# A relational graph layer with a routed FFN: 23 of its 1614 gathered tiles brought row by row by SyncE, x and its table moved in longer runs, and the selection begun before the last FFN block

## The reference

```
hx   = einsum('ni,rio->rno', h, weight)
agg  = segment_sum(hx[edge_type, src], dst)
x    = x + agg * sqrt(0.5) + h_bias + (h @ loop_weight) * sqrt(0.5)
z    = layernorm(x);   w = z @ wr + br
sel  = the 3124 nodes of largest w
y    = gelu(z @ w1 + b1) @ w2 + b2
out  = x + z + (y * w at the nodes of sel, 0 elsewhere)
```

## Time and profile before

| | us |
|---|---|
| median of 3 runs (lowest, highest) | 2587.57 (2576.79, 2591.49) |
| the profiled execution | 2560.34 |
| its span, first to last instruction | 2558.7 |
| first gather of GpSimd starts | 69.90 |
| first sum of TensorE starts | 84.99 |
| DVE's first step of the selection | 2498.37 |
| TensorE, GpSimd, DVE, ACT busy over the span | 1869.3, 1548.9, 776.9, 697.8 |

### The profile page before, as it was taken

The page is one execution under the profiler, slowest core; times in us unless marked ns, Lnnn a source line. Parts: engine busy times, 40 slices in busy tenths (PEclk is TensorE's granted clock), DMA queues, the critical chain, the costliest instruction groups (busy, mean ns, idle before and its releaser), DMA issues.

```text
span 2558.7 us, 25060 instructions
## 1 busy us (share of the span) xinstructions
PE 1869.3 (73%) x8680; PEld 1529.2 (60%) x8680; DVE 776.9 (30%) x1714; ACT 697.8 (27%) x1341; POOL 1548.9 (61%) x1737
## 2 busy tenths in 40 slices
PE   1237878777877877887877877877877877877881
PEld 0126657666665665665666666756656665666671
DVE  6112322232232232232232232232232232222337
ACT  5102223223222222222322322223223223223240
POOL 2666666666666666666666666666666666666500
PEclk9568888887887898887988988888988887887895
DMA  7533333333333333333333333333333333333315
GB/s 254 158 88 98 98 99 95 93 103 97 97 103 95 97 101 97 96 100 97 99 103 97 97 105 97 98 102 99 97 103 98 98 103 97 95 101 96 85 33 179
DMA packets 126598, 265.50 MB, mean 104 GB/s; under 512 B 30091, under 2 KB 73003, under 8 KB 126473
## 3 DMA queue, kind: packets, MB, share of 16 engines
q0 software_dynamic: 79168, 218.05, 29.6%
q1 hardware_dynamic: 47304, 45.83, 5.7%
HBM read 244.52 MB, written 19.25 MB: 103 GB/s over the span
## 4 chain that ended last, share of the span: by engine, by line
PE 55%; another core or an unknown queue 21%; issue 10%; ACT 8%; DVE 3%; DMA 1%; SPq 1%; DVEq 0%; POOL 0%; ACTq 0%; POOLq 0%
PE bank L642 21%; PE bank L670 13%; PE bank L688 7%; PE bank L696 7%; PE bank L652 4%; ACT hidden L541 2%; ACT stage L506 2%; PE bank L672 2%; ACT L541 1%; DMA acc<-in_edge_type 1%; DVE acc L1060 1%; ACT L528 1%; DMA w_sb<-in_L_ffn_w 1%; ACT normed_t L533 1%
## 5 line engine op out<-in xcount | busy, mean ns | idle before, releaser
L404 POOL DMA_INDIRECT messages<-normed_table,gather_rows x1614 | 1531.0, 949 | 854.3 <-issue 433.3
L642 PE MATMUL bank<-messages,onehot 128*128 128x256 f32 x3228 | 929.3, 423 | 124.9 <-issue 100.6
L642 PEld LDWEIGHTS bank<-messages,onehot 128*128 128x128 f32 x3228 | 642.6, 213 | 248.9 <-issue 179.0
L919 DVE SCALAR_TENSOR_TENSOR sums<-bank,regular,sums 128x256 f32 x538 | 259.9, 483 | 1657.4 <-remote 850.8
L506 ACT ACTIVATE stage<-bank 128x256 f32<-128x256 f32 x538 | 207.3, 388 | 1737.4 <-remote 1013.9
L652 PE MATMUL bank<-ident,stage 128*128 128x128 f32 x1076 | 234.4, 297 | 254.8 <-issue 158.8
L670 PE MATMUL bank<-rel_sb,closed 128*128 128x256 f32 x1568 | 361.6, 384 | 8.7 <-ACT closed L512 8.7
L652 PEld LDWEIGHTS bank<-ident,stage 128*128 128x128 f32 x1076 | 151.5, 152 | 336.1 <-issue 283.1
L688 PE MATMUL bank<-normed_t,w_sb 128*128 128x128 f32 x1568 | 240.0, 316 | 131.2 <-ACT normed_t L533 72.2
L670 PEld LDWEIGHTS bank<-rel_sb,closed 128*128 128x128 f32 x1568 | 302.3, 193 | 53.3 <-ACT closed L512 10.8
L688 PEld LDWEIGHTS bank<-normed_t,w_sb 128*128 128x128 f32 x1568 | 225.4, 229 | 147.1 <-ACT normed_t L533 85.6
(11 more groups left out here) (136 smaller groups left out, 519.8 us busy)
## 6 DMA issues: line engine op xcount, KB each, us to landing
messages<-normed_table,gather_rows POOLq DMA_INDIRECT x1614
normed_x<-normed_table SPq DMA_DIRECT2D x49, 128.0 KB
residual<-resid SPq DMA_DIRECT2D x49, 128.0 KB
x_block<-in_x SPq DMA_DIRECT2D x48, 128.0 KB
node_out<-acc SPq DMA_DIRECT2D x12, 512.0 KB
messages<-in_x POOLq DMA_DIRECT2D x6, 896.0 KB, 14.9
normed_table<-messages SPq DMA_DIRECT2D x6, 896.0 KB, 8.0
messages<-residual SPq DMA_DIRECT2D x6, 896.0 KB, 10.1
```

Source lines behind the costliest of these rows:

```text
L404: pool.indirect_dma_start(messages[0:EP, g % RING, j * D:(j + 1) * D], None, table, bass.IndirectOffsetOnAxis(ap=gather_rows[0:EP, g, j:j ...
L642: last = nc.tensor.matmul(banks[g % STAGES][:, 0:D], onehot[0:EP, g % SLOTS, j, :], messages[0:EP, slot, j * D:(j + 1) * D], start=(j == 0 ...
L919: V.scalar_tensor_tensor(sums[:, :, to], banks[TURNS[g % 2]][:, 0:D].rearrange("p (n m) -> p n m", m=W), regular[:, 0:1], sums[:, :, to], ...
```

## The change

Four edits are made together.

1. In 23 groups (every second closing group, from `closes[3]` to `closes[47]`) GpSimd issues two gathers instead of three. The third tile is brought by SyncE into `row_messages` (two buffers): `bring_rows` loads the tile's 128 indices, reads eight at a time into registers, and issues one transfer of 1 KB for each row; 64 rows stand ahead of `normed_x` in each of two successive blocks. TensorE waits for 128 transfers before the third product.
2. x and the table are moved with partition-major chunks, 7 rows in a run (7 KB) instead of 1 (1 KB). The table's content is the same.
3. `src` alone is loaded by SyncE, at once; `dst` and `edge_type` are loaded by GpSimd behind x, ahead of its constants. `index_stage` stands behind all chunks.
4. The selection starts when the last `w_all` is there. TensorE's FFN of the last block stands in pieces between the rounds' count products, and `ffn_leave` of that block behind the eighth round.

```diff
@@ top of the program
+    row_tiles = [closes[2 * k + 3] for k in range((NB - 3) // 2)]
+    row_tile_of = {g: k for k, g in enumerate(row_tiles)}
...
-        table_chunks = table.rearrange("(c v p) d -> c p v d", p=P, v=CH)
+        table_chunks = table.rearrange("(c p v) d -> c p v d", p=P, v=CH)
...
+        row_list = sb("row_list", [1, P], I32)
+        row_messages = sb("row_messages", [P, 2, D])
@@ SyncE
-            sp.wait_ge(pads_set, 3)
-            for a, to in ((dst, dst_s), (src, src_s), (edge_type, type_s)):
...
+            sp.wait_ge(pads_set, 1)
+            sp.dma_start(src_s[:, 0:full_tiles, :], src[0:full_tiles * P * GE].rearrange("(t p e) -> p t e", p=P, e=GE)).then_inc(src_in, 16)
...
+            def bring_rows(k, half):
+
+                first = row_tiles[k] * GE + (J - 1) * EP
+                if half == 0:
+                    sp.dma_start(row_list[0:1, :], src[first:first + P].rearrange("(o p) -> o p", o=1)).then_inc(row_list_in, 16)
+                    sp.wait_ge(row_list_in, 16 * (k + 1))
+                    if k >= 2:
+                        sp.wait_ge(summed, row_tiles[k - 2] + 1)
+                for p in range(half * P // 2, (half + 1) * P // 2, LOAD):
+                    registers = [sp.alloc_register(f"row{k}_{p + n}") for n in range(LOAD)]
+                    sp.load(registers, row_list[0:1, p:p + LOAD])
+                    for n in range(LOAD):
+                        row = sp.snap(registers[n], donate=True, min_val=0, max_val=N - 1)
+                        sp.dma_start(row_messages[p + n:p + n + 1, k % 2, :], table[bass.ds(row, 1), :]).then_inc(rows_in[k % 2], 16)
...
             for b in range(1, NB):
+                if (b - 1) // 2 < len(row_tiles):
+                    bring_rows((b - 1) // 2, (b - 1) % 2)
                 sp.wait_ge(loop_turned, b)
@@ GpSimd
-            x_chunks = x[0:(NCH - 1) * CH * P, :].rearrange("(c v p) d -> c p v d", p=P, v=CH)
+            nc.gpsimd.memset(closed_rows[P - 32:P, 0:CH, :], 0.0).then_inc(node_pad_set, 1)
+            x_chunks = x[0:last_first * P, :].rearrange("(c p v) d -> c p v d", p=P, v=CH)
...
+            for a, to in ((dst, dst_s), (edge_type, type_s)):
+                pool.dma_start(to[:, 0:full_tiles, :], a[0:full_tiles * P * GE].rearrange("(t p e) -> p t e", p=P, e=GE)).then_inc(edges_in, 16)
...
-                for j in range(J):
+                for j in range(J - (g in row_tile_of)):
                     pool.indirect_dma_start(messages[0:EP, g % RING, j * D:(j + 1) * D], None, table,
@@ ACT
-                    act.wait_ge(edges_in, 16 * 9)
+                    act.wait_ge(src_in, 16 * 3)
@@ TensorE
-                pe.wait_ge(gathered[slot], 16 * J * (g // RING + 1))
+                brought = sum(1 for t in row_tiles if t <= g and t % RING == slot)
+                pe.wait_ge(gathered[slot], 16 * (J * (g // RING + 1) - brought))
                 for j in range(J):
+                    tile = messages[0:EP, slot, j * D:(j + 1) * D]
+                    if j == J - 1 and g in row_tile_of:
+                        k = row_tile_of[g]
+                        pe.wait_ge(rows_in[k % 2], 16 * P * (k // 2 + 1))
+                        tile = row_messages[0:EP, k % 2, :]
...
             for r in range(8):
+                if r < 2:
+                    ffn_first(NB - 1, r * HC // 2, (r + 1) * HC // 2)
+                elif r >= 4:
+                    ffn_second(NB - 1, (r - 4) * HC // 4, (r - 3) * HC // 4)
                 pe.wait_ge(counts_in, r + 1)
@@ VectorE
-                dve.wait_ge(edges_in, 16 * 9)
+                dve.wait_ge(edges_in, 16 * 6)
...
-                if c == 2:
-                    index_stage()
+            index_stage()
             window_stage()
...
-            dve.wait_ge(ffn_done, 2 * NB + 1)
+            dve.wait_ge(ffn_step, FFN_STEPS * NB)
...
                 radix_round(4 + r, key_lo[:, :], 12 - 4 * r)
+            ffn_leave(NB - 1)
...
+            dve.wait_ge(ffn_done, 2 * NB + 1)
             for b in range(NB):
```

More of the change, by code:

```diff
@@ L83, in gnn_ffn_program @@
     assert len(closing) == NB and NG % 2 == 0 and all(closes[b] + LEAVE < closes[b + 2] for b in range(NB - 2))
+    row_tiles = [closes[2 * k + 3] for k in range((NB - 3) // 2)]
+    row_tile_of = {g: k for k, g in enumerate(row_tiles)}
+    assert len(row_tile_of) == len(row_tiles)
     SELECTED = max(1, int(0.5 * N)) - 1
@@ L209, in gnn_ffn_program @@
         consts = sem("consts")
+        src_in = sem("src_in")
         edges_in = sem("edges_in")
@@ L243, in gnn_ffn_program @@
         gathered = [sem(f"gathered{i}") for i in range(RING)]
+        row_list_in = sem("row_list_in")
+        rows_in = [sem(f"rows_in{i}") for i in range(2)]
         onehot_ready = sem("onehot_ready")
@@ L281, in gnn_ffn_program @@
         written = sem("written")
+        full_tiles = NG_FULL // P
+        rest = NG_FULL - full_tiles * P
+        last_first = (NCH - 1) * CH
+        last_whole = (N - last_first * P) // CH
+        last_rest = N - last_first * P - last_whole * CH
         block = ctx.enter_context(nc.Block())
@@ L286, in _ @@
         def _(sp):
-            full_tiles = NG_FULL // P
-            rest = NG_FULL - full_tiles * P
-            sp.wait_ge(pads_set, 3)
-            for a, to in ((dst, dst_s), (src, src_s), (edge_type, type_s)):
[L292 to L295, removed]
+            sp.wait_ge(pads_set, 1)
+            sp.dma_start(src_s[:, 0:full_tiles, :], src[0:full_tiles * P * GE].rearrange("(t p e) -> p t e", p=P, e=GE)).then_inc(src_in, 16)
+            sp.dma_start(src_s[0:rest, full_tiles, :], src[full_tiles * P * GE:NG_FULL * GE].rearrange("(p e) -> p e", e=GE)).then_inc(src_in, 16)
+            sp.dma_start(src_s[rest:rest + 1, full_tiles, 0:E - NG_FULL * GE],
+                         src[NG_FULL * GE:E].rearrange("(p e) -> p e", p=1)).then_inc(src_in, 16)
             sp.dma_start(loop_sb[:, :, :], loop_w.rearrange("(k p) o -> p k o", p=P)).then_inc(loop_in, 16)
@@ L639, in sum_group @@
                     pe.wait_ge(onehot_ready, g // 2 + 1)
-                pe.wait_ge(gathered[slot], 16 * J * (g // RING + 1))
+                brought = sum(1 for t in row_tiles if t <= g and t % RING == slot)
+                pe.wait_ge(gathered[slot], 16 * (J * (g // RING + 1) - brought))
                 for j in range(J):
+                    tile = messages[0:EP, slot, j * D:(j + 1) * D]
[3 more added lines that the diff above has]
+                        tile = row_messages[0:EP, k % 2, :]
                     last = nc.tensor.matmul(banks[g % STAGES][:, 0:D], onehot[0:EP, g % SLOTS, j, :],
-                                            messages[0:EP, slot, j * D:(j + 1) * D], start=(j == 0), stop=(j == J - 1))
+                                            tile, start=(j == 0), stop=(j == J - 1))
                 last.then_inc(summed, 1)
@@ L681, in ffn_turn, with ffn_first @@
                 last.then_inc(ffn_turned, 1)
[L683 to L686, removed]
+            def ffn_first(b, first=0, past=HC):
+                if first == 0:
+                    pe.wait_ge(ffn_norm_t, b + 2)
+                    pe.wait_ge(ffn_done, 2 * b + 1)
+                for m in range(first, past):
                     for k in range(KC):
@@ L690, in ffn_first, with ffn_second @@
                                                 start=(k == 0), stop=(k == KC - 1))
[L691 to L695, removed]
+                if past == HC:
+                    last.then_inc(ffn_up, 1)
+            def ffn_second(b, first=0, past=HC):
+                if first == 0:
+                    pe.wait_ge(ffn_gelu, b + 2)
+                for m in range(first, past):
                     last = nc.tensor.matmul(banks[5][:, 0:D], hidden[:, m, :], w2_sb[:, m, :],
                                             start=(m == 0), stop=(m == HC - 1))
-                last.then_inc(ffn_down, 1)
+                if past == HC:
+                    last.then_inc(ffn_down, 1)
             pe.wait_ge(rel_in, 16 * KC)
@@ L714, in _ @@
                     loop_turn(closing[g - LOOP])
-                if g - UP in closing:
+                if closing.get(g - UP, NB - 1) < NB - 1:
                     ffn_first(closing[g - UP])
-                if g - DOWN in closing:
+                if closing.get(g - DOWN, NB - 1) < NB - 1:
                     ffn_second(closing[g - DOWN])
             for r in range(8):
+                if r < 2:
+                    ffn_first(NB - 1, r * HC // 2, (r + 1) * HC // 2)
+                elif r >= 4:
+                    ffn_second(NB - 1, (r - 4) * HC // 4, (r - 3) * HC // 4)
                 pe.wait_ge(counts_in, r + 1)
@@ L1002, in _ @@
                     ffn_normalize(closing[g - NORM])
-                if g - LEAVE in closing:
+                if closing.get(g - LEAVE, NB - 1) < NB - 1:
                     ffn_leave(closing[g - LEAVE])
-            dve.wait_ge(ffn_done, 2 * NB + 1)
+            dve.wait_ge(ffn_step, FFN_STEPS * NB)
```

18 lines of the change are left out of this document (11 added, 7 removed).

## The result

| | before | after |
|---|---|---|
| median, us (lowest, highest, runs) | 2586.26 (2576.79, 2591.49, 4) | 2848.07 (2843.07, 2859.53, 4) |
| the profiled execution, us | 2560.34 | 2848.06 |
| its span, us | 2558.7 | 2846.4 |
| TensorE's mean granted clock | 0.844 | 0.826 |

The account below looks back on a forecast made before the run. The prediction took GpSimd's gather issue plus a nearly fixed number of pauses, with TensorE held while gathers flow, as the bound. 28.9 + 7.5 + 9 = 45.4, scaled 45.9: 2587.6 - 45.9 = 2542 us, range 2525 to 2600.

Parts of the forecast that it names:

- The bound of before: Loop: TensorE held while gathers flow; GpSimd's issue, 1614 x 1.256 us, plus 197 pauses adding 324.5 us, together 2352 us.
- first rival: Loop: TensorE alone paces it, so fewer gathers free nothing; 2571 us, chance 0.25.
- 23 gathers, 28.9 us: Loop, GpSimd's side: 23 gathers fewer at 1.256 us each save 28.9 us, 0 if TensorE alone paces.
- SyncE hidden at 28.5 us a block: Loop, SyncE's side: 64 rows take 28.5 us of a 47.6 us block; normed_x comes 6.5 us late, hidden.
- my own bound: Loop, SyncE: the rows stay hidden as long as one costs less than 0.65 us all in.
- the backlog row: SyncE: a one-row transfer behind a backlog took 1.98 us, giving at most 127 us for a block's rows.
- Third rival: Loop: a row costs SyncE over 0.65 us; at 1 us, 69 us a block, 970 us more; chance 0.04.
- Second rival: Loop: rows in flight keep up the hold on TensorE, lengthening 118 pauses by 189 us; 2731 us, chance 0.18.
- Start, 7.5 us: Program start: shorter ACT waits bring the first gather and sum earlier; 7.5 us taken, bounds 0 and 11.
- both waits of 8.33 and 2.60: Start, ACT's path: 8.33 us waiting for DVE in the index stage, 2.60 us for the edge types, to go.
- End, 9: Tail: selection starts at the last w_all instead of 10.4 us later; 9 us gained, bounds 6 and 10.4.
- the sum of 45.4 us: Whole kernel: gain of 28.9 for gathers, 7.5 for the start and 9 for the tail, scaled to 45.9.

Follow-up runs that it names:

- rows_32_4: Changed kernel with 11 row tiles instead of 23, 32 rows a block: 2565.9 us, 0.992 at the slower level; 0.982 at the faster.
- dropped: Changed kernel with the 23 tiles brought by nobody, their third product taking the second tile's rows: 2142.3 to 2143.1 us, 0.976 at the faster level.
- no_rows_4: Changed kernel without its first edit, GpSimd making all 1614 gathers: 2564.0 us, 0.992 at the slower level; 0.988 to 0.989 at the faster.
- rows_only: Kernel before with the first edit alone, start and end as before: 2166.8 us, 0.987 at the faster level.
- after_3: Changed kernel, unaltered, run again beside the kernel before: 2142.0 us, 0.976 at the faster level.

## Why the prediction was wrong, by its steps

- **The bound of before.** Right that TensorE is held while gathers flow: without gathers its block falls from 48 to 34 us, and the clear condition shows a loop in which only GpSimd's 1.256 us a gather counts. The reading "GpSimd's issue time plus a nearly fixed number of pauses" wasn't shown for the held condition: 11 gathers fewer gave nothing (rows_32_4). That fits the first rival, TensorE with its holds as the pace, but 32 slow rows a block were in the same run, and the 23 gathers alone weren't measured held.
- **23 gathers, 28.9 us.** 26.4 to 28.2 clear (dropped). Held not seen.
- **SyncE hidden at 28.5 us a block.** This is the step that failed. The undisturbed cost was nearly right: 32.4 us for 64 rows (0.41 a row, 0.78 a load in place of the 0.596 of DVE's). Held, it is 51.9 us and 3.4 for the rest, over the block of 48.15, so that `normed_x` comes late and TensorE waits for it. By my own bound all of it stays hidden up to 0.65 us a row, with 4.8 us for the loads beside it; measured are 51.9/64 = 0.81 with the loads in it, and about 0.71 with 8 x 0.78 us for them taken out. The upper end was as real: 121.7 us for the first half tile, 127 by the backlog row.
- **Why it failed.** I had seen that TensorE's results are held for up to 15 us, and took the hold to be TensorE's own. It reaches a run of SyncE's instructions too: a register check of 37 ns takes up to 1.4 us. The rows that I priced by were single instructions: those of the program's start, where no gather runs, and the 0.32 us of the earlier trace rows. That second one does stand amid gathers, and so do 139 transfers of SyncE in the kernel before, from 186.8 us to the last gather, of which none took over 0.333 us. For `normed_x`:

```profile
L334 SPq DMA_DIRECT2D normed_x<-normed_table x48: 319/320/327, 186.8 to 2437.0; - x48
```

  So the trace on record had rows from within the stretch, and they spoke for my price. It held no close run of SyncE instructions there, and TensorE, with 8680 matmuls the engine with by far the most instructions, was the one held. One instruction's time didn't price 64 in a row, and the far bound deserved more than 0.04. That the closeness of the instructions makes the difference is read from these rows; no run tests it by itself.
- **Third rival** (a row over 0.65 us, chance 0.04): the mechanism that happened, at 0.71 and not 1 (0.81 with the loads). Its law overshoots little: 46 x (55.3 - 48.15) = 329 us, for 307.8 measured from the first to the last store. **Second rival** (2731, 0.18) had a time nearer to the result and, by rows_32_4, the wrong mechanism for nearly all of the loss. The range of the prediction reached neither.
- **Start, 7.5 us.** 13.8 earlier at the first gather, over my upper bound of 11. ACT is done with x 13.1 us earlier (its last `closed` starts at 42.87 in place of 55.96): both waits of 8.33 and 2.60 are gone whole, the first chunk of x is there 1.06 us sooner (DVE starts at 9.60 in place of 10.66), and ACT no longer waits for the constants, so the 2 us counted for them weren't lost (GpSimd's six issues of x took 3.40 us in place of 5.84). The DMA engines didn't set the rest. Whether all of it lasts when held isn't told: no_rows_4 gains 20.4 with 9.8 of the end in it, within 15 to 26 by its interval.
- **End, 9.** 9.8 us (9.6 by the stretch behind the last gather, 96.2 in rows_only and 86.6 in no_rows).
- **By condition.** Clear, the sum of 45.4 us was measured as 52.2: the gathers gave a little less than their term, start and end 23.8 to 25.7 in place of 16.5. On the condition of its own trace it was wrong by sign.

The Trainium skill's rule to coalesce small transfers ("DMA: Bandwidth & Descriptors", Rules for kernel authors), which I weighed and set aside, pointed the right way in the held condition; in the clear one 64 rows a block cost nothing. The 2.0 us of the page are a fit to transfers that GpSimd issues (Anatomy of one DMA); from row to row SyncE needed 0.41 us undisturbed and 0.635 in the median when held.

## What to carry to other kernels

Work moved to an idle queue has to fit into the period of the loop, for behind it stand transfers that another engine wants in time; so leave slack for its worst price. If one engine is seen to be held by something without a name, don't take single instructions of another engine as proof that a long run of them is free there: the kernel before had none that was slow, and the first run of 64 was. Repeat the kernel before in each comparison: here it had two levels 16 to 18% apart, and the same edits gained 2.4% at one and lost 10% at the other. Only versions with slack on SyncE, rows_32 (0.982 clear, 0.992 held) and no_rows (0.988 to 0.989, 0.992), beat the kernel before at both levels, by under 2%, while the changed kernel as it is remains the best complete one in the clear condition.

## What the runs showed of the hardware

- The program had two levels, 2195 and 2550 to 2590 us, constant within a series. In the slower one close runs of instructions on TensorE and SyncE are held while GpSimd's indirect gathers flow: 64 one-row issues take 32.4 us without gathers, 51.9 beside gathers with pauses, 121.7 in the stretch in which GpSimd first fills its slots. In the faster one the same gathers, more densely issued (DMA share 0.39 against 0.31), hold nobody.
- The hold has a step. In the trace of the changed kernel on record 1149 of SyncE's 9438 distances from one instruction's start to the next lie within 0.02 us of 0.70 or 1.40; in after_3 13 do. Single instructions weren't stretched: SyncE's 139 transfers amid gathers in the kernel before took at most 0.333 us each.
- What sets the level, and by what way gathers reach the other queues, stays open. The DMA engines' own time for the gathers is the same at both levels. Every run here was recorded with its span and granted clock, so none tells whether the recording of the instructions has a part in the hold.
- SyncE reading eight register values takes 0.78 us; a one-row transfer with an address from a register 0.41 us from row to row.
